# Four block sums of h moved from DVE to GpSimd, with a new order of all steps, in a two-layer graph attention kernel

## The chip, the core and the metric

The kernel runs on one core of a Trainium2 chip. The metric is the device time of one execution in microseconds (us); the kernel before took 2622.17 us, the median of 3 runs (2616.54 to 2627.53). The engines are TensorE (PE; its weight loads are shown as PEld), VectorE (DVE), ScalarE (ACT), GpSimd (POOL) and SyncE (SP), which issues most DMAs. Each engine runs its own queue in order and waits on semaphores for the others.

## The reference

x is 64 graphs of 256 nodes with 512 features, adj a 256 x 256 matrix of zeros and ones.

```python
h = maximum(layernorm(x), 0)
q, k, v = h @ Wq + bq, h @ Wk + bk, h @ Wv + bv          # 8 heads of 64
scores = einsum('bihd,bjhd->bhij', q, k) / 8 + where(adj == 0, -1e9, 0)
x = x + einsum('bhij,bjhd->bihd', softmax(scores), v)    # layer 0
h = maximum(layernorm(x), 0)
q, k, v = h @ Wq1.T, h @ Wk1.T, h @ Wv1.T
rel = adj.T * (q @ k.T)
x = x + (rel / norm(rel, axis=2)) @ v                    # layer 1
```

## The kernel before, in words

The 64 graphs are worked on as 32 pairs (512 rows, four tiles of 128 each). Every fp32 operand of a product is split in two fp16 halves, high and low, and a product is three matmuls (high·high, high·low, low·high) where one would do. ACT makes the high half, then another engine subtracts it from the fp32 value: for h, the probabilities and the projections that is POOL.

The three projections of layer 0 ("q", "k", "v") use a scheme with seven products of half-size blocks where plain tiling has eight. For it h, which lies in `x_in` as four quarters a11, a12, a21, a22, gives seven blocks: three are quarters, four are sums of quarters. `h_sum` makes those four in place, one after the other, as `ln0_sum` 0 to 3: a22 = a21 + a22, a21 = a11 - a21, a11 = a22 - a11, a12 = a12 - a11. Sum 0 may run when the low half of block 4 (the old a22) is made, sum 1 when all four tiles are normalised, sum 2 after the low half of block 0, sum 3 after that of block 1. Each quarter is 128 x 512 fp32 as one instruction. The seven splits (`ln0_split` 0 to 6, in the block order 4, 0, 1, 2, 3, 5, 6) take high halves on ACT (L578), low halves on POOL (L501) and a DMA transpose into `h0t` from SP (L411). There are three places for the halves (`HALVES`), so split n waits for the transpose of split n-3.

Layer 0's attention has 16 units a pair (head and graph): scores on PE (L991, four groups of four units), "mask" on DVE (L837), "exp" and the high half on ACT (L645, L653), the low half on POOL (L523), a transpose by SP (L454), and "pv" on PE. After every four units DVE divides ("norm", L851) and POOL adds the result to x ("residual", L539). `residual` 0 waits until DVE has added the bias to all four tiles ("biased", L893). Layer 1 has the products "rv", "rq" (four each, 12 matmuls of 512 columns), "rel" and "out"; ACT takes the high half of rv and rq (L661) and DVE the low one (L859). All products of a pair except scores and pv share three PSUM banks `B` in turn, so a product waits until the product three before it has left its bank; for rv and rq that is the DVE instruction L859.

What stands where is decided by tables of slots. A pair starts every 26 slots (`PERIOD`); the tables give each step of a pair its slot, negative ones for the steps that run ahead of the pair's own period and ones above 26 for those that run in the next. `timetable` picks the tables of a pair (the first two and the last three have some of their own), and `in_order` sorts all steps into `TENSOR_PLAN` (PE) and `PLAN`. DVE, ACT, POOL and SP each walk through the same `PLAN` and take the steps that are theirs:

```python
                elif kind == "ln0_sum" and p > 0:
                    h_sum(n, p)
```

So in any period PE works on the projections of pair p, the attention of p and p-1 and layer 1 of p-1 and p-2, while h of pair p+1 is being made.

Of the kernel before, what the change touches and what calls it, by code (L numbers as in the profile page):

```python
# [5 lines left out]
def adjacency_attention_two_layers(  # L6
# [74 lines left out]
    LAYER1 = {"ln1_stats": [38, 38.25, 38.5, 38.5], "ln1_power": [38.75], "ln1_scale": [39.5],
              "ln1_apply": [41, 41, 41.25, 41.5], "ln1_split": [41, 41.25, 41.5, 41.75], "squares": [55.75, 59.25],
              "rel_scale": [56, 60], "rel_split": [57, 60.75]}
# [3 lines left out]
    OPENING = {("rq", 0): 2, ("rq", 1): 3, ("rq", 2): 4, ("rq", 3): 5}  # L87

    TURNED_AT = {("rv", 0): 19, ("rv", 1): 20, ("rv", 2): 21, ("rv", 3): 22, ("rel", 0): 28}


    PRODUCT_0 = {("q", 0): 0, ("q", 1): 1.3, ("q", 2): 1.6, ("q", 3): 2.5, ("q", 4): 3.5, ("q", 5): 4.5, ("q", 6): 5,
                 ("k", 0): 5.5, ("k", 1): 5.55, ("k", 2): 5.85, ("k", 3): 6.75, ("k", 4): 7.25, ("k", 5): 8,
                 ("k", 6): 8.5, ("v", 0): 11.25, ("v", 1): 11.55, ("v", 2): 12.35, ("v", 3): 13.75, ("v", 4): 14.5,
                 ("v", 5): 15.75, ("v", 6): 16}
# [971 lines left out]
```

## Time and profile before

| | before |
|---|---|
| median of 3 runs | 2622.17 us (2616.54 to 2627.53) |
| the profiled execution's own time | 2622.53 us |
| its span in the profile | 2620.7 us |
| PE busy | 2353.5 us (90%) |
| DVE busy | 2077.3 us (79%) |
| ACT busy | 1754.4 us (67%) |
| POOL busy | 1763.9 us (67%) |
| mean granted TensorE clock | 0.974 |

The span runs from the first to the last instruction; 1.8 us of the execution lie outside it. PE is the busiest engine, but a share averages over stages: what ends a wait in one stage is seen in the timeline of that stage. One pair takes some 79 us and the 32 overlap, so that nearly all of the span is one pattern, repeated.

### The profile page before, as it was taken

What the parts mean: (1) busy time and instruction counts of PE and PEld (TensorE: products, weight loads), DVE (VectorE), ACT (ScalarE), POOL (GpSimd) and SP (SyncE); (2) the same over time, 40 slices, a digit from 0 to 9 for tenths busy, and PEclk for the clock granted to TensorE, in tenths of its full rate; (3) what the DMA queues carried; (4) which work ended last, traced back from release to release, by engine and by line L of the source; (5) the groups of instructions that cost most, each with busy time, mean ns of one, the idle gap of its engine ahead of it and who ended that gap; (6) DMA issues with size and microseconds to landing.
All of it is one profiled execution on the core that took longest, in us unless ns stands there. A gap on an engine that the chain in (4) does not pass through costs nothing.

```text
span 2620.7 us, 62396 instructions
## 1 busy us (share of the span) xinstructions
PE 2353.5 (90%) x22708; PEld 1644.8 (63%) x22708; DVE 2077.3 (79%) x5261; ACT 1754.4 (67%) x4318; POOL 1763.9 (67%) x1511
## 2 busy tenths in 40 slices
PE   5789999998999899999889999999999999999996
PEld 3656676666676665666656766666766656766663
DVE  6778877788888788877788887888787888787863
ACT  3676766776666676666666766666666766766762
POOL 2767776767676766766666766676676776666761
PEclk8899999999999999999999999999999999999998
DMA  5666766776777676666766766766666866766752
GB/s 165 126 129 130 143 139 131 138 150 130 139 148 126 137 151 129 138 137 123 149 133 136 147 126 130 153 132 139 146 128 132 156 132 138 146 128 131 142 120 66
DMA packets 1040353, 354.87 MB, mean 135 GB/s; under 512 B 987440, under 2 KB 987696, under 8 KB 1040048
## 3 DMA queue, kind: packets, MB, share of 16 engines
q1 hardware_dynamic: 1037264, 345.65, 65.6%
q10 hardware_dynamic: 2784, 5.24, 0.5%
q8 instruction: 180, 2.95, 0.5%
q14 instruction: 125, 1.02, 0.1%
HBM read 73.93 MB, written 33.55 MB: 41 GB/s over the span
## 4 chain that ended last, share of the span: by engine, by line
DVE 38%; PE 37%; issue 9%; POOL 6%; ACT 4%; DMA 2%; DVEq 0%; SPq 0%; ACTq 0%
PE B L908 33%; DVE whole L817 4%; DVE stats L707 4%; DVE rel_halves L871 3%; DVE probs L837 3%; DVE u L828 3%; DVE ln_work L695 2%; PE O L908 2%; DVE x_in L735 2%; PE S L991 2%; DVE x_in L739 2%; DVE x_in L743 2%; POOL x_res L539 2%; POOL halves L523 1%; DVE ln_work L699 1%
## 5 line engine op out<-in xcount | busy, mean ns | idle before, releaser
L523 POOL TENSOR_TENSOR halves<-probs,halves 128x512 f16<-128x512 f32 x512 | 618.7, 1211 | 325.5 <-ACT halves L653 322.5
L645 ACT ACTIVATE probs<-probs,neg_max 128x256 f32<-128x256 f32 x1024 | 506.8, 496 | 280.8 <-DVE neg_max L837 280.8
L908 PE MATMUL B<-h1t,wm 128*128 128x512 f16 x1488 | 371.0, 403 | 85.0 <-DVE rv L859 85.0
L501 POOL TENSOR_TENSOR h_halves<-x_in,h_halves 128x512 f16<-128x512 f32 x224 | 298.9, 1340 | 146.3 <-ACT h_halves L578 146.3
L908 PE MATMUL B<-wvt,h1t 128*128 128x512 f16 x1488 | 339.0, 380 | 51.7 <-DVE rv L859 34.6
L837 DVE CUSTOM_DVE_ANT_0 probs<-S,mask 128x256 f32<-128x256 f32 x1024 | 379.6, 416 | 5.5 <-PE S L991 2.6
L908 PE MATMUL B<-h0t,wq 128*128 128x256 f16 x2688 | 329.2, 275 | 24.5 <-ACT u L625 15.0
L653 ACT ACTIVATE halves<-probs 128x512 f16<-128x512 f32 x512 | 322.7, 630 | 16.2
L908 PE MATMUL B<-h0t,wk 128*128 128x256 f16 x2688 | 309.0, 273 | 11.5 <-DVE rel L865 11.5
L908 PE MATMUL B<-wv,h0t 128*128 128x256 f16 x2688 | 314.9, 273 | 1.3 <-DVE u L828 1.3
L908 PEld LDWEIGHTS B<-h1t,wm 128*128 128x128 f16 x1488 | 143.9, 103 | 267.4 <-DVE rv L859 99.8
L908 PEld LDWEIGHTS B<-h0t,wq 128*128 128x128 f16 x2688 | 256.1, 99 | 62.1 <-ACT u L625 15.3
L908 PEld LDWEIGHTS B<-wv,h0t 128*128 128x128 f16 x2688 | 257.7, 98 | 50.3 <-issue 7.0
L908 PEld LDWEIGHTS O<-v,probs_t 128*128 128x128 f16 x6144 | 237.2, 99 | 82.0 <-POOL v L520 17.4
L908 PEld LDWEIGHTS B<-h0t,wk 128*128 128x128 f16 x2688 | 256.3, 98 | 48.2 <-DVE rel L865 19.8
L908 PEld LDWEIGHTS B<-wvt,h1t 128*128 128x128 f16 x1488 | 138.4, 98 | 226.2 <-DVE rv L859 49.4
L908 PE MATMUL O<-v,probs_t 128*128 128x64 f16 x6144 | 255.5, 194 | 16.0 <-POOL v L520 6.3
L828 DVE TENSOR_TENSOR u<-B,u 128x512 f32<-128x512 f32 x288 | 196.6, 683 | 62.9 <-PE B L908 62.8
L539 POOL TENSOR_TENSOR x_res<-x_res,attn 128x512 f32<-128x512 f32 x124 | 157.7, 1272 | 98.7 <-DVE x_res L893 55.4
L908 PE MATMUL B<-rv,rel_t 128*128 128x512 f16 x768 | 190.8, 386 | 30.8 <-DVE u L828 21.9
L508 POOL TENSOR_TENSOR h_halves<-h,h_halves 128x512 f16<-128x512 f32 x128 | 148.5, 1160 | 101.1 <-ACT h_halves L592 101.0
L991 PE MATMUL S<-k_st,q_st 64*128 64x256 f16 x3072 | 191.7, 271 | 25.9 <-DVE neg_max L837 25.6
(114 smaller groups left out, 4090.2 us busy)
## 6 DMA issues: line engine op xcount, KB each, us to landing
x_in<-in_x_dram SPq DMA_DIRECT2D x132, 256.0 KB, 3.9
out_dram<-result SPq DMA_DIRECT2D x128, 256.0 KB, 3.4
x_res<-in_x_dram SPq DMA_DIRECT2D x124, 256.0 KB, 3.2
probs_t<-halves SPq DMA_TRANSPOSE x512, 2.9
h0t<-h_halves SPq DMA_TRANSPOSE x228, 3.2
h1t<-h_halves SPq DMA_TRANSPOSE x124, 3.7
rq<-in_L_gnn_Wq_dram ACTq DMA_DIRECT2D x4, 256.0 KB, 5.1
x_res<-in_L_gnn_Wk_dram ACTq DMA_DIRECT2D x4, 256.0 KB, 5.8
```

The costliest lines, as they stand in the source:

```text
L501: nc.gpsimd.tensor_tensor(halves_by_column(step, 1), by_column(h_block(SPLIT_ORDER[n])), halves_by_column(step, 0), ALU.subtract).then_inc ...
L508: nc.gpsimd.tensor_tensor(h_halves[:, place, 1, :], h[:, n % 2, :], h_halves[:, place, 0, :], ALU.subtract).then_inc(h_low[1], 1)
L523: nc.gpsimd.tensor_tensor(halves[:, n % RING, 1, :], probs[:, (UNITS * p + n) % SOFT, :, :].rearrange("p t n -> p (t n)"), halves[:, n % R ...
L539: nc.gpsimd.tensor_tensor(cols, cols, attn[:, :, :].rearrange("p (t e) d -> p t (e d)", e=2), ALU.add).then_inc(residual, 1)
L645: ins = nc.scalar.activation(probs[:, soft, i, :], probs[:, soft, i, :], ACT.Exp, bias=neg_max[:, soft, i:i + 1], scale=-1.0, accum_out=ro ...
L653: nc.scalar.activation(halves[:, n % RING, 0, :], probs[:, (UNITS * p + n) % SOFT, :, :].rearrange("p t n -> p (t n)"), ACT.Copy).then_inc ...
L707: ins = nc.vector.bn_stats(stats[:, layer, t, :], src[:, t, :])
L817: ins = nc.vector.scalar_tensor_tensor(whole[:, c % 2, t, :], now[:, t, :], b[:, f + t:f + t + 1], before[:, t, :], ALU.add, ALU.add)
L828: nc.vector.tensor_tensor(u[:, 1 if n == 3 else 0, :, :].rearrange("p t n -> p (t n)"), product[:, :], before, ALU.add).then_inc(u_done, 1)
L837: ins = nc.vector.tensor_tensor_reduce(out=probs[:, soft, i, :], in0=S[n % 4][:, i, :], in1=mask[:, i, :], scale=SCORE, scalar=BIG, op0=AL ...
L908: ins = nc.tensor.matmul(dst, left(i), right(j), start=(n == 0), stop=(n == len(pairs) - 1))
L991: ins = nc.tensor.matmul(S[2 * g + e][:, i, :], q_st[own, n, hq, col(g * NT + i)], k_st[own, n, hk, col(g, N)], start=(t == 0), stop=(t == ...
```

## The change

`h_sum` is taken out of DVE's part and made a helper that takes the engine. The four sums of the first pair, in the setup, are still called on DVE; those of all other pairs are issued by POOL, at their place in `PLAN`. The waits of each sum are the same as before. The slots of nearly every step change in the tables for all pairs, for the first two and for the last three. The tables `OUT_29`, `PRODUCT_30` and so on of the last three pairs keep the old numbers or get new ones, where before they repeated those of all pairs.

```diff
-    SCORED = [8.75, 12.75, 20.0, 26.5]
-    MASKED = [9, 12, 16.25, 19, 23.0, 25.5, 29, 31]
+    SCORED = [8.25, 13.75, 22.0, 28.0]
+    MASKED = [9, 12, 16.0, 19.75, 23.75, 26.0, 27.5, 30]
...
-              "ln0_apply": [-8.5, -8.25, -7.5, -7.25], "ln0_sum": [-7, -7, -6.5, -5.25],
+              "ln0_scale": [-9], "ln0_apply": [-8.5, -8, -7.5, -7.25], "ln0_sum": [-7, -7, -6.5, -4.25],
...
+        def h_sum(eng, engine, n, pair):
+
+            a11, a12, a21, a22 = [quarter(x_in, i, j) for i in range(2) for j in range(2)]
+            low = BLOCKS * pair + 1
+            if n == 0:
+                eng.wait_ge(h_low[0], low + SPLIT_ORDER.index(4))
+                ins = engine.tensor_tensor(a22, a21, a22, ALU.add)
...
+            ins.then_inc(summed_blocks, 1)
+
         @block.sync
...
                     ln_power(1, p + 1)
+                elif kind == "ln0_sum" and p > 0:
+                    h_sum(pool, nc.gpsimd, n, p)
                 elif kind == "ln0_split" and p > 0:
                     h0_low_half(n, p)
...
             for n in range(4):
-                h_sum(n, 0)
+                h_sum(dve, nc.vector, n, 0)
...
-                elif kind == "ln0_sum" and p > 0:
-                    h_sum(n, p)
```

Below, rows of the two programs' order of instructions, in the middle of the run. The line numbers of the changed kernel differ: L862 is the old L859, L894 the old L893, L847 the old L844, L523 the old L501, L545 the old L523, L563 the old L539, L909 the old L908, L992 the old L991; L413, L417, L421 and L425 are the four sums. DVE, where rv2, rv3 and rq0 leave their banks, before:

```order
L893 TENSOR_TENSOR x_res<-x_res,bv 128x512
L735 TENSOR_TENSOR x_in<-x_in 128x2x256
L739 TENSOR_TENSOR x_in<-x_in 128x2x256
L743 TENSOR_TENSOR x_in<-x_in 128x2x256
L893 TENSOR_TENSOR x_res<-x_res,bv 128x512
L859 TENSOR_TENSOR rv<-B,rv 128x512
L893 TENSOR_TENSOR x_res<-x_res,bv 128x512
L859 TENSOR_TENSOR rv<-B,rv 128x512
L747 TENSOR_TENSOR x_in<-x_in 128x2x256
L844 RECIPROCAL row_inv<-row_sum 128x8
L859 TENSOR_TENSOR rq<-B,rq 128x512
```

DVE at the same place, changed:

```order
L894 TENSOR_TENSOR x_res<-x_res,bv 128x512
L862 TENSOR_TENSOR rv<-B,rv 128x512
L894 TENSOR_TENSOR x_res<-x_res,bv 128x512
L862 TENSOR_TENSOR rv<-B,rv 128x512
L847 RECIPROCAL row_inv<-row_sum 128x8
L894 TENSOR_TENSOR x_res<-x_res,bv 128x512
L862 TENSOR_TENSOR rq<-B,rq 128x512 x2
```

The four sums are gone, one biased tile (x_res<-x_res,bv) stands ahead of each of rv2 and rv3 and one behind, and rq1's low half now stands ahead of the four masks that follow.

POOL from the first split of h to the residual, before (h_halves are low halves of h, halves those of the probabilities of units 6 and 7, the row with attn is residual 0):

```order
L501 TENSOR_TENSOR h_halves<-x_in,h_halves 128x512 x2
L523 TENSOR_TENSOR halves<-probs,halves 128x512
L501 TENSOR_TENSOR h_halves<-x_in,h_halves 128x512
L523 TENSOR_TENSOR halves<-probs,halves 128x512
L539 TENSOR_TENSOR x_res<-x_res,attn 128x4x128
L523 TENSOR_TENSOR halves<-probs,halves 128x512
L501 TENSOR_TENSOR h_halves<-x_in,h_halves 128x512
L523 TENSOR_TENSOR halves<-probs,halves 128x512
```

POOL at the same place, changed:

```order
L523 TENSOR_TENSOR h_halves<-x_in,h_halves 128x512
L413 TENSOR_TENSOR x_in<-x_in 128x2x256
L417 TENSOR_TENSOR x_in<-x_in 128x2x256
L523 TENSOR_TENSOR h_halves<-x_in,h_halves 128x512
L421 TENSOR_TENSOR x_in<-x_in 128x2x256
L523 TENSOR_TENSOR h_halves<-x_in,h_halves 128x512
L545 TENSOR_TENSOR halves<-probs,halves 128x512
L563 TENSOR_TENSOR x_res<-x_res,attn 128x4x128
L545 TENSOR_TENSOR halves<-probs,halves 128x512
L425 TENSOR_TENSOR x_in<-x_in 128x2x256
```

Three sums now stand ahead of unit 6 and the fourth behind unit 7, and the residual has moved up between the two units.

PE from rv0 to the unit behind rq3, before (wvt is a product rv, wm one of rq, O a unit of pv, S the scores):

```order
L908 MATMUL B<-wvt,h1t 128x512 x12
L908 MATMUL O<-v,probs_t 128x64 x12
L908 MATMUL B<-wvt,h1t 128x512 x36
L991 MATMUL S<-k_st,q_st 128x256 x24
L908 MATMUL O<-v,probs_t 128x64 x12
L908 MATMUL B<-h1t,wm 128x512 x24
L908 MATMUL O<-v,probs_t 128x64 x12
L908 MATMUL B<-h1t,wm 128x512 x12
L908 MATMUL O<-v,probs_t 128x64 x12
L908 MATMUL B<-h1t,wm 128x512 x12
L908 MATMUL O<-v,probs_t 128x64 x12
```

PE at the same place, changed:

```order
L909 MATMUL B<-wvt,h1t 128x512 x24
L909 MATMUL O<-v,probs_t 128x64 x12
L909 MATMUL B<-wvt,h1t 128x512 x24
L909 MATMUL B<-h1t,wm 128x512 x12
L909 MATMUL O<-v,probs_t 128x64 x12
L992 MATMUL S<-k_st,q_st 128x256 x24
L909 MATMUL B<-h1t,wm 128x512 x24
L909 MATMUL O<-v,probs_t 128x64 x24
L909 MATMUL B<-h1t,wm 128x512 x12
L909 MATMUL O<-v,probs_t 128x64 x12
```

The scores and one pv, which stood ahead of rq0, stand behind it now, and a pv has moved from between rq1 and rq2 to behind rq2.

PE at the very end of the program, before: the last pair's rv (wvt), rq (wm), rel and out.

```order
L908 MATMUL B<-wvt,h0t 128x512 x48
L908 MATMUL B<-h0t,wm 128x512 x48
L908 MATMUL B<-h0t,rq 128x256 x48
L908 MATMUL B<-rv,rel_t 128x512 x24
```

PE at the same place, changed:

```order
L909 MATMUL B<-h0t,wm 128x512 x48
L909 MATMUL B<-h0t,rq 128x256 x24
L909 MATMUL B<-wvt,h0t 128x512 x24
L909 MATMUL B<-h0t,rq 128x256 x24
L909 MATMUL B<-wvt,h0t 128x512 x24
L909 MATMUL B<-rv,rel_t 128x512 x24
```

The last pair takes rq first, and its rv in two parts behind each rel.

## Rows read from the trace of the kernel before

**Rows 1.** The page, parts 1 and 4: busy time; chain that ended last.

```profile
PE 2353.5 (90%) x22708; PEld 1644.8 (63%) x22708; DVE 2077.3 (79%) x5261; ACT 1754.4 (67%) x4318; POOL 1763.9 (67%) x1511
...
DVE 38%; PE 37%; issue 9%; POOL 6%; ACT 4%; DMA 2%; DVEq 0%; SPq 0%; ACTq 0%
```

**Rows 2.** Waits, 400 to 2400 us: waiting line <- releaser: us, times, longest.

```profile
PE B L908 <- DVE rv L859: 103.7, 50, 2.8
...
PE B L908 <- DMA h1t<-h_halves: 14.7, 28, 1.7
```

**Rows 3.** Timeline, PE, one pair: start us, us, line, tiles, [idle before].

```profile
1337.46 2.75 PE L908 MATMUL B<-wvt,h1t 128*128 128x512 f16 x12 [1.72 <-DMA h1t<-h_halves]
...
1347.04 2.76 PE L908 MATMUL B<-wvt,h1t 128*128 128x512 f16 x12 [1.29 <-DVE rv L859]
1350.35 1.49 PE L991 MATMUL S<-k_st,q_st 64*128 64x256 f16 x24 [0.55 <-DVE neg_max L837]
...
1357.72 2.76 PE L908 MATMUL B<-h1t,wm 128*128 128x512 f16 x12 [2.84 <-DVE rv L859]
...
1363.26 0.51 PE L908 MATMUL O<-v,probs_t 128*128 128x64 f16 x12
...
1372.00 0.51 PE L908 MATMUL O<-v,probs_t 128*128 128x64 f16 x12
```

**Rows 4.** Timeline, DVE, the same stretch.

```profile
1350.72 1.65 DVE L735 TENSOR_TENSOR x_in<-x_in 128x512 f32<-128x512 f32 x1
...
1355.42 1.64 DVE L893 TENSOR_TENSOR x_res<-x_res,bv 128x512 f32<-128x512 f32 x1
1356.98 0.68 DVE L859 TENSOR_TENSOR rv<-B,rv 128x512 f16<-128x512 f32 x1
```

**Rows 5.** The first sum by line: ns min/median/max, first and last start.

```profile
L735 DVE TENSOR_TENSOR x_in<-x_in x32: 679/1648/1651, 18.3 to 2452.4; 128x512 f32<-128x512 f32 x32
```

**Rows 6.** Groups by line: count | busy us, mean ns | idle before.

```profile
L539 POOL TENSOR_TENSOR x_res<-x_res,attn 128x512 f32<-128x512 f32 x124 | 157.7, 1272 | 98.7 <-DVE x_res L893 55.4 <-DVE attn L851 43.3
...
L893 DVE TENSOR_TENSOR x_res<-x_res,bv 128x512 f32<-128x512 f32 x124 | 115.3, 930 | 0.0
...
L735 DVE TENSOR_TENSOR x_in<-x_in 128x512 f32<-128x512 f32 x32 | 51.8, 1617 | 7.5 <-POOL h_halves L501 7.5
```

**Rows 7.** Timeline, POOL, the same stretch.

```profile
1347.70 1.16 POOL L501 TENSOR_TENSOR h_halves<-x_in,h_halves 128x512 f16<-128x512 f32 x1 [2.99 <-ACT h_halves L578]
...
1351.90 1.49 POOL L523 TENSOR_TENSOR halves<-probs,halves 128x512 f16<-128x512 f32 x1
...
1354.91 1.60 POOL L523 TENSOR_TENSOR halves<-probs,halves 128x512 f16<-128x512 f32 x1
1358.34 1.26 POOL L539 TENSOR_TENSOR x_res<-x_res,attn 128x512 f32<-128x512 f32 x1 [1.83 <-DVE x_res L893]
```

**Rows 8.** Timeline, DVE, a sum of the first pairs.

```profile
95.20 0.68 DVE L735 TENSOR_TENSOR x_in<-x_in 128x512 f32<-128x512 f32 x1
```

**Rows 9.** Transposes of the probabilities: ns in the SP queue; us to landing.

```profile
L454 SPq DMA_TRANSPOSE probs_t<-halves x512: 1231/1237/2549, 73.2 to 2554.9; - x171
...
DMA to landing us min/median/max: 2.7/2.9/6.8
```

**Rows 10.** Timeline, PE, the wait at rq1 in the first pair.

```profile
171.77 4.19 PE L908 MATMUL B<-h1t,wm 128*128 128x512 f16 x12 [2.84 <-DVE rv L859]
```

**Rows 11.** Two windows: busy us (x) by engine, PEclk, DMA share, GB/s.

```profile
171.00:176.00 5.00, 4.23 (x20) 1.74 (x21) 5.00 (x14) 0.63 (x2) 3.61 (x3) 0.66 0.37 76
1357.00:1362.00 5.00, 4.28 (x31) 2.17 (x32) 5.00 (x14) 0.63 (x3) 3.66 (x3) 1.00 0.45 92
```

**Rows 12.** Timeline, PE, the last pair's products.

```profile
2574.01 12.31 PE L908 MATMUL B<-wvt,h0t 128*128 128x512 f16 x48 [9.54 <-DMA h0t<-h_halves]
...
2598.19 5.40 PE L908 MATMUL B<-h0t,rq 128*128 128x256 f16 x48 [1.51 <-DVE rq L859]
2609.27 8.27 PE L908 MATMUL B<-rv,rel_t 128*128 128x512 f16 x24 [5.68 <-issue]
```

More of the change, by code:

```diff
@@ L81, in adjacency_attention_two_layers @@
[L81 to L95, printed above, removed]
@@ new lines, in adjacency_attention_two_layers @@
+    LAYER0 = {"x_in": [-25, -24.25, -24.25, -19.25], "ln0_stats": [-14.25, -12, -11.75, -9.5], "ln0_power": [-10],
+              "ln0_scale": [-9], "ln0_apply": [-8.5, -8, -7.5, -7.25], "ln0_sum": [-7, -7, -6.5, -4.25],
+              "ln0_split": [-7.5, -6.5, -6.5, -4, -3.25, 0.25, 0.75], "x_res": [7.5, 12.25, 15.25, 15.25],
+              "biased": [18, 20.5, 21, 22], "residual": [20, 24.75, 31.5, 35.5]}
+    LAYER1 = {"ln1_stats": [38, 38.25, 38.25, 38.25], "ln1_power": [38.5], "ln1_scale": [39.25],
+              "ln1_apply": [41, 41, 41.5, 41.75], "ln1_split": [41, 41.25, 41.5, 41.75], "squares": [54.75, 59.5],
+              "rel_scale": [56, 60], "rel_split": [57, 60.5]}
@@ new lines, in adjacency_attention_two_layers @@
+    OPENING = {('rq', 0): 2, ('rq', 1): 3, ('rq', 2): 4, ('rq', 3): 5}
+    TURNED_AT = {('rv', 0): 19.0, ('rv', 1): 19.25, ('rv', 2): 20.25, ('rv', 3): 24.5, ('rel', 0): 25.75}
+    PRODUCT_0 = {("q", 0): 0, ("q", 1): 1.05, ("q", 2): 1.35, ("q", 3): 2.25, ("q", 4): 3.25, ("q", 5): 3.5,
[3 rows of a table added]
+    SCORED_0 = [8.5, 13.0, 21.25, 27.0]
+    MASKED_0 = [9.25, 12, 15.5, 20.0, 23.25, 25.75, 27.5, 30.25]
+    MULTIPLIED_0 = [14.5, 15, 16.25, 16.25, 22, 22.25, 23.75, 25.25, 28.75, 29, 30, 31, 34, 34.25, 35.5, 35.5]
@@ new lines, in adjacency_attention_two_layers @@
+    LAYER0_0 = {"x_res": [10.75, 11.5, 12.5, 13.25], "biased": [16.75, 19.25, 20.75, 22.75],
+                "residual": [22.75, 25.5, 32, 35.5]}
+    PRODUCT_1 = {("q", 0): -2, ("q", 1): -0.2, ("q", 2): 0.35, ("q", 3): 2.25, ("q", 4): 2.25, ("q", 5): 4.5,
[3 rows of a table added]
+    LAYER0_1 = {"x_in": [-24, -23.75, -22.75, -22.25], "ln0_stats": [-16.75, -12.75, -12.75, -10], "ln0_power": [-10],
+                "ln0_scale": [-9.5], "ln0_apply": [-9, -8.75, -8, -7.5], "ln0_sum": [-7.5, -6.75, -6, -4.75],
+                "ln0_split": [-8, -7, -6.25, -3.75, -3, -2, 0.25]}
@@ L117, in adjacency_attention_two_layers @@
                   ("k", 6): 8.5, ("v", 0): 11.25, ("v", 1): 11.55, ("v", 2): 12.35, ("v", 3): 13.75, ("v", 4): 14.5,
[2 rows of a table removed]
-                  ("rel", 1): 56.75, ("out", 0): 61, ("out", 1): 62.5, ("out", 2): 66.75, ("out", 3): 67.25}
[2 rows of a table added]
+                  ("out", 0): 53, ("out", 1): 54, ("out", 2): 55, ("out", 3): 56}
     SCORED_31 = [8.75, 12.75, 20.0, 26.5]
@@ L404, in need @@
                 eng.wait_ge(semaphore, value)
+        def h_sum(eng, engine, n, pair):
[4 more added lines that the diff above has]
+                ins = engine.tensor_tensor(a22, a21, a22, ALU.add)
+            elif n == 1:
+                eng.wait_ge(ln_done[0], TILES * (pair + 1))
+                eng.wait_ge(summed_blocks, 4 * pair + 1)
+                ins = engine.tensor_tensor(a21, a11, a21, ALU.subtract)
+            elif n == 2:
+                eng.wait_ge(h_low[0], low + SPLIT_ORDER.index(0))
+                eng.wait_ge(summed_blocks, 4 * pair + 2)
+                ins = engine.tensor_tensor(a11, a22, a11, ALU.subtract)
+            else:
+                eng.wait_ge(h_low[0], low + SPLIT_ORDER.index(1))
+                eng.wait_ge(summed_blocks, 4 * pair + 3)
+                ins = engine.tensor_tensor(a12, a12, a11, ALU.subtract)
+            ins.then_inc(summed_blocks, 1)
         @block.sync
```

54 lines of the change are left out of this document (10 added, 44 removed), and 18 rows, old and new, of tables (PRODUCT_0, PRODUCT_1, PRODUCT_31, PRODUCT_AT).

## The prediction

> **What bounds the kernel now.** I read the page first. PE is busy 90% of the span, DVE 79%, and the chain that ended last lies on these two in equal parts, 38% on DVE and 37% on PE [rows 1]. So PE's work sets most of the time and DVE the rest; the question is where PE waits. The list of waits answers it: from 400 to 2400 us PE waited 103.7 us, in 50 waits, for the DVE instruction that takes rv's low half out of its bank, and 14.7 us for the transposes of layer 1's h; nothing else comes near [rows 2].
>
> The timeline of one pair shows where that is. PE waits 1.72 us ahead of rv0, 1.29 ahead of rv3, 0.55 ahead of the third group of scores and 2.84 at 1357.72 ahead of rq1 [rows 3]. That last one needs the bank of rv2. DVE starts rv2's low half only at 1356.98, and ahead of it stand three of the four block sums, from 1350.72 to 1355.42, and one biased tile of 1.64 [rows 4]. So the sums stand in the one stretch in which PE waits for DVE. The length of a pair comes from the same wait, which is at 171.77 in the first pair [rows 10] and at 1357.72 fifteen pairs later: 1185.95 / 15 = 79.06 us. It occurs 30 times: the first sum is there 32 times [rows 5], of which one is in the setup and one, the second pair's, has no layer 1 beside it.
>
> **What the change removes.** On DVE a sum takes 1.62 us in the mean [rows 6] and 1.65 beside a busy POOL, against 0.68 where nothing is in its way [rows 4, 8]. Gone are at most 4 x 1.65 = 6.6 us a pair of DVE, and 4.7 of it ahead of rv2. DVE would come to rv2 after one biased tile, at 1350.7 + 1.64 = 1352.4, and the bank would be free at 1353.1. PE, without the waits of 0.55 and 2.84, comes to rq1 at 1357.72 - 3.39 = 1354.33. The wait of 2.84 goes, with 1.2 us to spare. The 0.55 goes as well, since these scores now stand behind rq0 and one pv, 3 us later, and the masks that they wait for don't. **Term 1: -3.39 us a pair**, between -3.39 and -1.7 (if ACT, whose high half of rv2 comes first, delays it by half).
>
> **What it adds.** POOL has no row for such a sum. The nearest is residual, same shape, fp32 out: 1.27 us in the mean [rows 6]; a low half takes 1.16 alone and 1.49 to 1.60 beside DVE's sums [rows 7]. I take 1.27; the ends are 1.16 and 1.65. POOL is not idle enough for it to be free everywhere. What stands behind the sums on POOL are the low halves of the probabilities, then SP's transposes, then pv on PE.
>
> - Unit 6. Before, its low half ends at 1351.90 + 1.49 = 1353.39, and PE wants it at 1363.26 [rows 3, 7]: plenty. Changed, POOL has four low halves and three sums to make from 1347.70 on, and the first split stands behind rv1's high half on ACT, some 0.55 later. 1347.70 + 0.55 + 4 x 1.16 + 3 x 1.27 = 1356.70, and 0.44 more for each of two biased tiles that come between (1.60 against 1.16): 1357.6. The transpose lands 2.9 us after its issue [rows 9], at 1360.5. PE now comes there at 1363.26 - 3.39 = 1359.87. A new wait of 0.6.
> - Unit 8. Behind unit 6 POOL has the residual, unit 7, the fourth sum, two splits and unit 8: 2 x 1.27 + 4 x 1.16 = 7.18, with one more tile of DVE between 7.62. That is 1365.2, landing at 1368.1, or 1369.4 if SP is still issuing the one ahead, 1.24 each [rows 9]. PE came there at 1372.00 [rows 3]; it now comes 3.39 earlier, without the last scores (1.42 from the row of 1.49) ahead of it, and 0.6 later again: 1367.8. A new wait of 0.3 to 1.6; I take 0.8.
>
> **Term 2: +1.4 us a pair.** The lower end: nothing contends, unit 6 lands at 1356.70 + 2.9 = 1359.6 and unit 8 at 1366.8, both ahead of PE: 0. The upper end: every POOL instruction takes 1.60. Unit 6 ends at 1347.70 + 0.55 + 7 x 1.60 = 1359.45 and lands at 1362.35 (wait 2.5), unit 8 six instructions later at 1369.05, landing at 1371.95 against 1369.7 (2.3): +4.8.
>
> DVE also pays: its biased tiles take 0.93 in the mean and 1.64 beside POOL [rows 4, 6]. If all four meet the busier POOL that is 4 x 0.71 = 2.8 us a pair, less than half of what it was relieved of, and the tile ahead of rv2 is in the sum above.
>
> What speaks against the move is a rule of the Trainium skill (GPSIMD Engine Reference, Engine selection): elementwise work on two inputs belongs on VectorE, as GpSimd is about twice as slow. In this trace 1.27 stands against 0.68, the ratio the page gives, but in the place where the sums stand DVE takes 1.65. By the page a sum would be 2 x 0.68 = 1.36, which makes term 2 larger by under 0.4. The 1.65 agrees with the SBUF page (Who interferes with whom): a DVE instruction with two SBUF inputs and a GpSimd one that reads SBUF exclude each other, and the later fully waits.
>
> **Term 3, the clock.** In the first pair the 12 matmuls behind the wait of 2.84 took 4.19 us, with a granted clock of 0.66 in that window; fifteen pairs later, behind the same wait, 2.76 at 1.00 [rows 3, 10, 11]. So such a wait can cost up to 1.43 us more, in some pairs and not in others. With no wait of that length left, part of it comes back: between 0 and -1.43; **I take -0.6 us a pair**.
>
> **The rest of the order.** From rq1 to rv0 PE has no wait of over a microsecond, and the new slots there trade places of products and pv; I see nothing that removes the waits of 1.72 ahead of rv0 and 1.29 ahead of rv3, which hang on the layer-norm chain. I take 0, with ends of -1 and +1 a pair. The first two pairs: 0, with 4 us to both sides.
>
> **The last pair.** Before, rv starts at 2574.01, as soon as the first of four tiles is transposed; rel waits 1.51 and out 5.68, and the 24 matmuls of out take 8.27 [rows 12], against 5.2 at the rate of the steady pairs (12 matmuls of the same width take 2.6 of the 2.75 that the row of rq shows, 0.216 each) [rows 3]. Changed, rq goes first and needs all four tiles: three more transposes of 1.24 and some waiting for the three places, 3.7 to 5 us later, say 4.3. In exchange rv fills the wait for rel's halves: 5.68 less 1 that I leave, and out at the full rate, 3.1. Together 4.3 - 4.7 - 3.1 = -3.5, between -8 and +4.
>
> **The sum.** -3.39 + 1.4 - 0.6 = -2.59 a pair, x 30 = -77.7, and -3.5 at the end: -81.2. The profiled execution took 2622.53 us (its span is 2620.7, the rest lies outside it), 0.4 from the median of 2622.17. 2622.5 - 81.2 = 2541.3. **I predict 2541 us**, about 3% faster.
>
> **Rivals.**
>
> *POOL hides the sums.* Term 2 is 0 and the clock gives back all: -3.39 - 1.43 = -4.82 a pair, 2622.5 - 144.6 - 3.5 = 2474; with half of the clock's part, 2496. For it: POOL is 67% busy and waited 1.83 us ahead of the residual alone [rows 1, 7]. Against it: the sums stand in its densest stretch. Between 2474 and 2510.
>
> *The wait only moves.* rq1 no longer waits, but another chain that runs once round a pair sets its length: residual 3, layer 1's stats, its transposes (the 1.72 ahead of rv0) or the scale chain behind rv3's 1.29, both of which pass through DVE instructions that a busier POOL lengthens. If 0.5 us of 3.39 is left: 2622.5 - 15 - 3.5 = 2604; if nothing, 2619. For it: DVE and PE share the chain evenly [rows 1]. Against it: both of these waits begin far behind rq1, and 14.7 us in 25 pairs is the smaller part [rows 2].
>
> *POOL becomes the bound: slower.* Three sums and the residual stand ahead of unit 7, and the residual waits on POOL until the fourth biased tile, which now stands behind rv3's low half on DVE. If POOL's instructions are all of 1.60, term 2 is +4.8: -3.39 + 4.8 = +1.4 a pair, x 30 = +42, and 2622.5 + 42 - 3.5 = 2661. It decides from the point where units 6 and 8 together cost PE more than 3.4 us, that is where POOL is 2.9 us later than I have it. For it: 1.60 was measured beside DVE's sums. Against it: just those are gone.
>
> That the order does not change is excluded by the rows of both programs.
>
> **How the numbers follow.** My forecast's case has 62%, with a range of its own of 2515 to 2570 (1 us a pair to either side). POOL hides the sums: 13%. The wait moves: 15%, half of it above 2604. POOL bounds: 10%. The range for 8 in 10 goes from 2488 to 2604: it leaves out the slower rival, half of the moved wait and the lowest part of the first rival, 19% together. Half a per cent, 13 us, is about what a measurement here can tell. Faster by more: 62 + 13 + 8 = 83%. Within it: 7 of the moved wait and 1 of the last, 8%. Slower: 9%.
>
> **What would show it.** Right: the wait for rv's bank ahead of rq1 is gone, while those ahead of rv0 and rv3 stay; four sums a pair on POOL of about 1.27 us; new waits of under a microsecond of pv for the transposes of the probabilities; a pair of 76.5 us; fewer stretches of lower granted clock; a last out without the wait of 5.68. Wrong: pv waits of 2 us and more (term 2), sums on POOL of 1.6 and more, a pair still of 78 to 79 us with longer waits ahead of rv0 or rv3, or new waits of the projections for a bank, since I took 0 for all the other moves.

## The result

The changed kernel took **2539.66 us**, the median of 4 runs (2537.17 to 2541.73). The kernel before took 2620.98 in the same comparison (4 runs, 2616.54 to 2627.53). The ratio is 0.9687, with a 95% interval of 0.9665 to 0.971: about 3% faster. The prediction was 2541, with a range of 2488 to 2604.

The profiled execution took 2541.73 us, with a span of 2539.9. The page, parts 1 and 4, to be laid beside [rows 1]:

```profile
PE 2327.8 (92%) x22708; PEld 1645.1 (65%) x22708; DVE 1899.1 (75%) x5137; ACT 1755.9 (69%) x4318; POOL 1877.2 (74%) x1635
...
PE 34%; DVE 25%; POOL 18%; issue 9%; DMA 7%; ACT 5%; SPq 2%; ACTq 0%; DVEq 0%; POOLq 0%
```

POOL has the 124 instructions that DVE lost, and 113 us more to do; DVE has 178 less. Of the chain that ended last 18% now lie on POOL, where it was 6%. PE is busy 26 us less with the same 22708 matmuls, as the mean granted clock rose from 0.974 to 0.985.

PE's waits from 400 to 2300 us, a stretch of 24.9 pairs (waiting line <- releaser: us, times, longest):

```profile
PE O L909 <- DMA probs_t<-halves: 42.7, 40, 2.8
PE B L909 <- DVE rv L862: 30.0, 25, 1.4
...
PE B L909 <- DMA h1t<-h_halves: 18.1, 33, 2.1
```

Before, the first of these was not there and the second stood at 103.7 us, in 50 waits over 2000 us [rows 2]. One pair on PE (start us, us, tiles, [idle before]), against [rows 3]:

```profile
1298.25 5.34 PE L909 MATMUL B<-wvt,h1t 128*128 128x512 f16 x24 [1.58 <-DMA h1t<-h_halves]
...
1307.83 2.76 PE L909 MATMUL B<-wvt,h1t 128*128 128x512 f16 x12 [1.30 <-DVE rv L862]
1310.43 2.75 PE L909 MATMUL B<-h1t,wm 128*128 128x512 f16 x12
1313.02 0.51 PE L909 MATMUL O<-v,probs_t 128*128 128x64 f16 x12
1313.47 1.48 PE L992 MATMUL S<-k_st,q_st 64*128 64x256 f16 x24
1314.88 5.35 PE L909 MATMUL B<-h1t,wm 128*128 128x512 f16 x24
...
1321.49 0.52 PE L909 MATMUL O<-v,probs_t 128*128 128x64 f16 x12 [0.91 <-DMA probs_t<-halves]
```

The waits ahead of rv0 (1.58, was 1.72) and rv3 (1.30, was 1.29) stay. Those ahead of the third scores and of rq1 are gone: rq0, pv, the scores and then rq1 and rq2 run without a gap. The new one is ahead of pv of unit 6. POOL in the same stretch, against [rows 7]:

```profile
1308.83 1.16 POOL L523 TENSOR_TENSOR h_halves<-x_in,h_halves 128x512 f16<-128x512 f32 x1 [3.33 <-ACT h_halves L602]
1310.07 1.27 POOL L413 TENSOR_TENSOR x_in<-x_in 128x512 f32<-128x512 f32 x1
1311.49 1.54 POOL L417 TENSOR_TENSOR x_in<-x_in 128x512 f32<-128x512 f32 x1
...
1314.22 1.70 POOL L421 TENSOR_TENSOR x_in<-x_in 128x512 f32<-128x512 f32 x1
...
1317.00 1.61 POOL L545 TENSOR_TENSOR halves<-probs,halves 128x512 f16<-128x512 f32 x1
1318.56 1.26 POOL L563 TENSOR_TENSOR x_res<-x_res,attn 128x512 f32<-128x512 f32 x1
```

From split 0 (1308.83) to the end of unit 6's low half (1318.61) POOL does seven instructions with hardly a gap. The residual behind them no longer waits for the biased tiles, as it did for 1.83. Three sums and DVE's biased tile in the groups by line, against [rows 6] (count | busy us, mean ns | idle before):

```profile
L894 DVE TENSOR_TENSOR x_res<-x_res,bv 128x512 f32<-128x512 f32 x124 | 112.3, 905 | 0.0
...
L421 POOL TENSOR_TENSOR x_in<-x_in 128x512 f32<-128x512 f32 x31 | 52.9, 1705 | 2.4
L417 POOL TENSOR_TENSOR x_in<-x_in 128x512 f32<-128x512 f32 x31 | 47.4, 1530 | 4.3
L413 POOL TENSOR_TENSOR x_in<-x_in 128x512 f32<-128x512 f32 x31 | 39.5, 1274 | 2.4
```

On DVE, before, these four sums took 51.8, 46.2, 45.7 and 42.4 us in 32 instructions each, 1.45 us in the mean. On POOL the four groups together (the last one 39.2 us) have a mean of 1.44: in their own places the sums are as long on one engine as on the other.

**Where the 80.8 us of span went.** The first sum of the third pair starts at 164.77 before and at 163.14 after, that of the last one at 2452.36 and at 2372.4: 78.88 and 76.18 us a pair, 2.70 less, 78.3 over 29 pairs. The head gives 1.6, and what follows the last sum 0.8 (168.3 and 167.5). So nearly all of it is in the pairs.

### The profile page after: what moved, and what is told of

It is laid out like the page before. It is cut to its first block, busy times and chain, and to the rows that moved or that the text cites. A ratio compares the mean times of both kernels' runs of the same rounds, so it can differ in the third digit from the quotient of the medians.

```text
span 2539.9 us, 62396 instructions
## 1 busy us (share of the span) xinstructions
PE 2327.8 (92%) x22708; PEld 1645.1 (65%) x22708; DVE 1899.1 (75%) x5137; ACT 1755.9 (69%) x4318; POOL 1877.2 (74%) x1635
## 3 DMA queue, kind: packets, MB, share of 16 engines
q14 instruction: 126, 1.03, 0.2%
## 4 chain that ended last, share of the span: by engine, by line
PE 34%; DVE 25%; POOL 18%; issue 9%; DMA 7%; ACT 5%; SPq 2%; ACTq 0%; DVEq 0%; POOLq 0%
PE B L909 29%; DMA probs_t<-halves 5%; DVE stats L731 4%; POOL h_halves L523 4%; POOL halves L545 3%; PE O L909 3%; DVE ln_work L721 3%; DVE ln_work L719 3%; POOL x_res L563 3%; DVE probs L840 2%; DVE u L831 2%; POOL x_in L421 2%; PE S L992 2%; POOL x_in L417 2%; SPq L434 2%
## 5 line engine op out<-in xcount | busy, mean ns | idle before, releaser
L545 POOL TENSOR_TENSOR halves<-probs,halves 128x512 f16<-128x512 f32 x512 | 607.4, 1187 | 185.4 <-ACT halves L677 183.0
L909 PE MATMUL B<-wvt,h1t 128*128 128x512 f16 x1488 | 337.7, 380 | 55.4 <-DVE rv L862 34.7
L909 PE MATMUL B<-h0t,wq 128*128 128x256 f16 x2688 | 325.3, 276 | 26.1 <-ACT u L649 15.4
L523 POOL TENSOR_TENSOR h_halves<-x_in,h_halves 128x512 f16<-128x512 f32 x224 | 258.1, 1164 | 114.1 <-ACT h_halves L602 114.1
L909 PE MATMUL B<-h1t,wm 128*128 128x512 f16 x1488 | 339.7, 382 | 0.0
L909 PEld LDWEIGHTS O<-v,probs_t 128*128 128x128 f16 x6144 | 233.5, 98 | 148.4 <-DMA probs_t<-halves 58.8
L909 PE MATMUL O<-v,probs_t 128*128 128x64 f16 x6144 | 259.8, 194 | 69.5 <-DMA probs_t<-halves 63.6
L909 PE MATMUL B<-wv,h0t 128*128 128x256 f16 x2688 | 310.2, 273 | 0.1
L909 PE MATMUL B<-h0t,wk 128*128 128x256 f16 x2688 | 304.1, 273 | 0.3 <-DVE whole L820 0.3
L909 PEld LDWEIGHTS B<-h0t,wq 128*128 128x128 f16 x2688 | 256.9, 99 | 58.7 <-ACT u L649 15.7
L909 PEld LDWEIGHTS B<-wvt,h1t 128*128 128x128 f16 x1488 | 139.0, 98 | 229.0 <-DVE rv L862 49.5
L909 PEld LDWEIGHTS B<-wv,h0t 128*128 128x128 f16 x2688 | 257.5, 98 | 43.6 <-issue 7.0
L909 PEld LDWEIGHTS B<-h0t,wk 128*128 128x128 f16 x2688 | 260.5, 98 | 30.6 <-DVE whole L820 0.6
L909 PEld LDWEIGHTS B<-h1t,wm 128*128 128x128 f16 x1488 | 141.6, 98 | 169.3 <-issue 9.9
L831 DVE TENSOR_TENSOR u<-B,u 128x512 f32<-128x512 f32 x288 | 197.1, 684 | 51.8 <-PE B L909 50.8
L542 POOL TENSOR_TENSOR k_st<-whole,k_st 128x512 f16<-128x512 f32 x128 | 151.1, 1180 | 89.7 <-ACT k_st L660 89.7
L909 PE MATMUL B<-rv,rel_t 128*128 128x512 f16 x768 | 188.1, 382 | 25.2 <-DVE u L831 24.1
L992 PE MATMUL S<-k_st,q_st 64*128 64x256 f16 x3072 | 192.2, 272 | 9.8 <-DVE neg_max L840 8.2
```

Source lines behind the costliest of these rows:

```text
L523: nc.gpsimd.tensor_tensor(halves_by_column(step, 1), by_column(h_block(SPLIT_ORDER[n])), halves_by_column(step, 0), ALU.subtract).then_inc ...
L542: nc.gpsimd.tensor_tensor(dst(1), whole[:, c % 2, :, :], dst(0), ALU.subtract).then_inc(whole_low, 1)
L545: nc.gpsimd.tensor_tensor(halves[:, n % RING, 1, :], probs[:, (UNITS * p + n) % SOFT, :, :].rearrange("p t n -> p (t n)"), halves[:, n % R ...
L831: nc.vector.tensor_tensor(u[:, 1 if n == 3 else 0, :, :].rearrange("p t n -> p (t n)"), product[:, :], before, ALU.add).then_inc(u_done, 1)
L909: ins = nc.tensor.matmul(dst, left(i), right(j), start=(n == 0), stop=(n == len(pairs) - 1))
L992: ins = nc.tensor.matmul(S[2 * g + e][:, i, :], q_st[own, n, hq, col(g * NT + i)], k_st[own, n, hk, col(g, N)], start=(t == 0), stop=(t == ...
```

## The experiments

All were run in three rounds beside the kernel before, which took 2618.93, 2619.17 and 2627.47 us in its three comparisons. So a difference of a few us between two versions of different rounds says little by itself. The waits quoted are all of PE, from 400 to 2300 us. The diffs are cut to the lines that matter; `...` marks what is left out.

### The two parts of the change apart

**New slots, sums on DVE.** The changed kernel with the sums back on their old engine:

```diff
-                elif kind == "ln0_sum" and p > 0:        # in POOL's walk through PLAN
-                    h_sum(pool, nc.gpsimd, n, p)
+                elif kind == "ln0_sum" and p > 0:        # in DVE's
+                    h_sum(dve, nc.vector, n, p)
```

> The changed kernel with all its new slots, but the four sums back on DVE. My theory (the sums belong off DVE, the slots only make room): on DVE sums 0 to 2 now stand ahead of the masks of units 6 and 7 and of rv2's low half, 4.7 us of them, so PE waits 2 to 4 us a pair at the third scores or at rq1, and the time is 2590 to 2660 us. Rival (the new slots carry the gain, the engine is nothing): 2540 us, within 10.

Measured: 2605.07 us (2599.15 to 2606.37), ratio 0.994 (0.9919 to 0.9961). The new slots alone bring 14 of the 80 us.

```profile
PE S L992 <- DVE neg_max L838: 54.1, 25, 2.2
```

The long wait is still there, once a pair, and has moved: it is ahead of the third scores (2.17 us at 1344.85), which wait for masks. On DVE these stand behind sum 2, and sum 2 behind POOL:

```profile
1341.70 1.63 DVE L421 TENSOR_TENSOR x_in<-x_in 128x512 f32<-128x512 f32 x1 [1.05 <-POOL h_halves L523]
1343.25 0.41 DVE L838 CUSTOM_DVE_ANT_0 probs<-S,mask 128x256 f32<-128x256 f32 x1
```

The rival, that the new order makes the gain by itself, falls. It is less the length of the sums that holds DVE up here: the four take 117.7 us in this trace, 0.92 each, against 186.1 before. DVE also stands idle 31.4 us for POOL ahead of sum 2, with the masks behind it.

**Old slots, sums on POOL.** The reverse: the tables of the kernel before with the sums in POOL's walk.

```diff
-    LAYER0 = {... "ln0_sum": [-7, -7, -6.5, -4.25],
-              "ln0_split": [-7.5, -6.5, -6.5, -4, -3.25, 0.25, 0.75], ...
+    LAYER0 = {... "ln0_sum": [-7, -7, -6.5, -5.25],
+              "ln0_split": [-8, -7, -6.5, -4, -3.25, -2.25, 0], ...      # and all other tables of before
```

> The kernel before with all its old slots, the four sums on POOL. My theory: PE's wait of 2.84 us ahead of rq1 is gone, the 0.55 ahead of the third scores stays, and POOL takes back under 1 us a pair as two of the sums stand ahead of unit 6 and three ahead of unit 7: 2550 to 2575 us. Rival (the new slots carry the gain): 2610 to 2622 us, with another wait in the place of the one removed.

Measured: **2522.01 us** (2519.52 to 2522.65), ratio 0.9625 (0.9593 to 0.9657). That is below the expected range, and 17.7 faster than the changed kernel. The engine move alone brings 97 us; the new slots, worth 14 with the sums on DVE, cost 17.7 once they are on POOL. Its waits:

```profile
PE B L908 <- DVE rv L861: 41.5, 50, 1.4
...
PE S L991 <- DVE neg_max L839: 14.7, 27, 0.6
...
PE O L908 <- DMA probs_t<-halves: 0.4, 2, 0.3
```

Pv waits 0.4 us in all. The reason stands on POOL:

```profile
1300.17 1.58 POOL L416 TENSOR_TENSOR x_in<-x_in 128x512 f32<-128x512 f32 x1
1301.72 1.60 POOL L522 TENSOR_TENSOR h_halves<-x_in,h_halves 128x512 f16<-128x512 f32 x1
1303.28 1.15 POOL L544 TENSOR_TENSOR halves<-probs,halves 128x512 f16<-128x512 f32 x1
1304.40 1.26 POOL L420 TENSOR_TENSOR x_in<-x_in 128x512 f32<-128x512 f32 x1
```

Unit 6's low half (L544) comes ahead of the third sum and its split; in the changed kernel it comes behind both. It ends 17.1 us after the start of rv0 here and 20.4 there, while PE comes to unit 6 some 22 to 23 us after it in both. The price is a wait of 0.37 us ahead of rq1 and the old 0.55 ahead of the third scores. Together its waits are 94.7 us against 113.1, and a pair is (2352.6 - 96.0) / 30 = 75.22 us long, against (2372.4 - 93.0) / 30 = 75.98 with the same count in the changed kernel.

**Sums later on DVE.** The kernel before, in which the sums stay on DVE but stand behind rv3's low half:

```diff
-"ln0_sum": [-7, -7, -6.5, -5.25]
+"ln0_sum": [-5.2, -5.15, -5.1, -5.05]
```

> The kernel before, sums on DVE, with their slots alone moved behind rv3's low half. My theory, that rq1 waits only because the sums stand ahead of rv2: the 2.84 us are gone, but the sums now stand ahead of the masks of units 8 and 9 and hold up ACT's splits 3 to 6, which takes back 1 to 2 us a pair: 2565 to 2605 us. Rival (DVE simply has too much work, so that it must go to another engine): 2615 us or more.

Measured: 2588.39 us (2587.61 to 2588.75), ratio 0.988 (0.9848 to 0.9912).

```profile
PE S L991 <- DVE neg_max L837: 37.9, 50, 1.0
PE B L908 <- DVE rv L859: 35.2, 46, 1.4
```

The wait for rv, 96.6 us in this stretch of the kernel before, is down to 35.2 without POOL's help: it was the sums' place ahead of rv2. But DVE is as full as before and hands the time to the scores, in pieces of a microsecond or less. The place alone is worth 31 us; the other 66 of the 97 take the other engine. Of the 31 much is clock, not waiting: the group of rq matmuls went from 371.0 to 341.9 us, while all waits together went only from 152.4 to 135.9.

### POOL's order and load

**Unit 6 first.** If pv's wait is the order on POOL, unit 6's low half ahead of split 1, sum 2 and split 2 should end it:

```diff
-    MASKED = [9, 12, 16.0, 19.75, 23.75, 26.0, 27.5, 30]
+    MASKED = [9, 12, 16.0, 19.25, 23.75, 26.0, 27.5, 30]
```

> The changed kernel with the slot of the masks of units 6 and 7 at 19.25 where it had 19.75, so that on POOL unit 6's low half stands ahead of one split, the third sum and another split, and unit 7's behind the residual as before. My theory, that PE's new waits of 0.9 us and more ahead of pv of unit 6 come from what stands ahead of it on POOL: they go, and the time falls by 1 to 1.5 us a pair to 2495 to 2515 us. Rival (the waits are transposes that queue on SP or collide, whatever POOL's order): 2535 to 2545 us, the waits where they were.

Measured: 2546.43 us (2540.73 to 2548.19), ratio 0.9713 (0.9692 to 0.9734). A miss by 31, near the rival's time, but not for its reason.

```profile
PE B L909 <- DVE rv L862: 52.6, 47, 1.4
...
PE O L909 <- DMA probs_t<-halves: 19.5, 25, 2.2
```

pv's wait halves (42.7 to 19.5), and rv's grows by the same (30.0 to 52.6): a new one of 0.82 us stands ahead of rq1. The order on POOL was indeed the cause at unit 6. In the changed kernel some 31 of the 42.7 us are ahead of unit 6; here none of the 19.5 is: 14.8 are ahead of unit 8 and the rest ahead of unit 7. The sum of all waits is 114.1 against 113.1. On DVE, rv2's low half now waits 3.35 us for ACT's high half:

```profile
1316.86 0.69 DVE L862 TENSOR_TENSOR rv<-B,rv 128x512 f16<-128x512 f32 x1 [3.35 <-ACT rv L685]
```

In the changed kernel ACT makes it at 1312.90, between the exponentials of units 6 and 7, and DVE waits 1.62; here it comes behind both, at 1316.25. One slot put right does not take the wait out: the slot moves the unit on every engine, and the wait changes places.

**Spare work on POOL, new slots.** Three additions of 128 x 128 a pair ahead of split 1's low half, into a tile that nobody reads:

```diff
+                    if n == 1:
+                        for part in range(3):
+                            need(pool, spare_done, 3 * (p - 1) + part)
+                            nc.gpsimd.tensor_tensor(spare[:, :], ident[:, :], ident[:, :],
+                                                    ALU.add).then_inc(spare_done, 1)
                     h0_low_half(n, p)
```

> The changed kernel with three spare additions of 128x128 on POOL for each pair, ahead of the second split of h, which compute nothing that is used (about 1.3 us of POOL a pair, taken from the 0.29 us of the 128x128 select in the setup and the semaphore between them). My theory (POOL is what PE waits for in this stretch): the 1.3 us come out nearly whole in the waits of pv, +30 to +42 us: 2570 to 2582 us. Rival (POOL has room left): 2540 to 2550 us.

Measured: 2607.76 us (2604.62 to 2612.47), ratio 0.9953 (0.9936 to 0.997), 68 above the changed kernel. The 93 additions took 37.1 us (399 ns each).

```profile
PE O L916 <- DMA probs_t<-halves: 68.9, 26, 3.8
```
```profile
1510.07 0.82 PE L916 MATMUL O<-v,probs_t 128*128 128x64 f16 x12 [2.58 <-DMA probs_t<-halves]
1510.70 4.11 PE L916 MATMUL B<-h1t,wm 128*128 128x512 f16 x12
```
```profile
1510.00:1515.00 5.00, 4.93 (x37) 2.49 (x38) 0.69 (x1) 2.60 (x8) 3.72 (x4) 0.66 0.71 142
```

pv waits 68.9 us in 24.3 pairs, against 42.7 in 24.9: 1.12 more a pair, 34 over thirty. The other half is the clock: behind the wait the 12 matmuls take 4.11 us, with a granted clock of 0.66 in those 5 us (the third value from the end; part at 1.2 GHz, which is 0.5, and part at 2.4), where they take 2.75 at 1.00. The group of all rq matmuls went from 339.7 to 373.5 us, +33.8. The mechanism was as expected, its size was not (26 us above the range): the clock had been left out. Behind unit 6's wait the 12 matmuls of rq3 were slow, 3.94 us or more instead of 2.75, in 21 of 25 pairs here; in the changed kernel in 2 of 25.

**The same, twice instead of three times.**

```diff
-                        for part in range(3):
+                        for part in range(2):
```

> The changed kernel with two spare additions a pair in place of three (0.8 us of POOL a pair by the 399 ns that one took). Three cost 68 us, 2.3 a pair, for 1.2 us of work; rq's matmuls took 34 us longer in all with it, 409 ns in place of 382. My theory (the rest is the clock, which falls behind a wait of PE of over 2 us): 0.8 x 30 = 24 us of waits and a smaller share of slow stretches, 2565 to 2590 us, with rq's matmuls between 382 and 409. Rival (the cost is in proportion, each addition 23 us): 2585 us, with rq's matmuls at 400.

Measured: 2576.34 us (2572.88 to 2578.83), ratio 0.9813 (0.9775 to 0.9851), +36.7. pv waits 57.1 us, the rq group takes 367.1 us (404 ns a matmul). The 12 matmuls of rq3 were slow in 16 of 25 pairs. The first two additions cost 18.3 us each and the third, 12.4 us of POOL, another 31.4: the time is in the theory's range, and the rival's even 23 each does not hold. The theory's words on waits of over 2 us go further than the traces: in the changed kernel the wait of 2.38 at 555.75 was followed by slow matmuls and that of 2.20 at 633.54 was not.

**Spare work on POOL, old slots.** The same three additions in the kernel with the old slots and POOL's sums.

> The same spare additions in the kernel with the old slots and the sums on POOL (2522 us). There PE waited 0.4 us in 25 pairs for the probabilities. My theory (under the old slots unit 6 stands further up on POOL and PE comes to it behind one product fewer, so there is room): under +10 us, 2522 to 2532 us. Rival (POOL is as tight there): +30 us, 2550 us or more.

Measured: 2562.2 us (2561.93 to 2562.27), ratio 0.9777 (0.9756 to 0.9797), 40 above its own base.

```profile
L559 POOL TENSOR_TENSOR spare<-ident 128x128 f32<-128x128 f32 x93 | 50.4, 542 | 4.9
...
L915 PE MATMUL B<-h1t,wm 128*128 128x512 f16 x1488 | 341.6, 379 | 11.1 <-DVE rv L868 11.1
```
```profile
PE S L998 <- DVE neg_max L846: 39.7, 49, 1.2
```

50.4 us of POOL's work, 40 of the span: POOL has no room under the old slots either, and that theory falls. It reaches PE by way of the scores (14.7 to 39.7 us, none over 1.2), and the rq matmuls stay at 379 ns. So the same load costs 28 us less here. The clock's part of the other, some 34 us, is near that.

### Giving one sum back to DVE

If POOL sets the pace, one sum less should bring something.

```diff
-                elif kind == "ln0_sum" and p > 0:
+                elif kind == "ln0_sum" and p > 0 and n not in (3,):      # POOL
+                elif kind == "ln0_sum" and p > 0 and n in (3,):          # DVE
+                    h_sum(dve, nc.vector, n, p)
```

**Sum 3, old slots with the new end:**

> The best so far (old slots, sums on POOL, new slots for the last two pairs, 2518.7 us) with the fourth sum back on DVE, where it stands behind rv3's low half and no longer ahead of anything that PE waits for at rq1. My theory, after the spare load showed POOL to set the pace in this stretch under either slots: 1.27 us a pair come off POOL and most of it off the time, 2485 to 2500 us. Rival (the load acted through its place ahead of unit 6 alone, and the fourth sum stands behind unit 7): 2515 to 2522 us. A second rival (DVE takes it back, since the sum takes 1.4 us there beside POOL): 2525 us or more.

Measured: 2531.33 us (2530.65 to 2533.73), ratio 0.9648 (0.9616 to 0.9679), 13 slower than with it on POOL (2518.66, the version with the new end, below). The theory missed by 31; the second rival had it.

```profile
L424 DVE TENSOR_TENSOR x_in<-x_in 128x512 f32<-128x512 f32 x32 | 51.2, 1600 | 15.8 <-POOL h_halves L522 15.7
```

On DVE the sum takes 1600 ns, more than the 1270 on POOL, and DVE idles 15.7 us ahead of it. PE's waits for the masks went from 14.6 to 23.2 us.

**Sum 3, new slots:**

> The changed kernel (2539.7 us) with the fourth sum back on DVE. The waits of pv come at unit 6, ahead of the fourth sum on POOL, and at unit 8 and 9, behind it. If POOL's whole chain sets the pace: 2505 to 2520 us. If only what stands ahead of unit 6 does: the small waits at unit 8 go, 2532 to 2540 us.

Measured: 2534.7 us (2532.71 to 2538.02), ratio 0.966 (0.9628 to 0.9692), 5 below the changed kernel with ranges that touch: not clear. It stood behind unit 6 on POOL, and pv waits 39.6 instead of 42.7. POOL's whole chain does not set the pace. The time fits the second expectation, but its reason does not: the waits at unit 8 stay, up to 1.62 us.

**Sum 1, old slots with the new end** (`n in (1,)`):

> As the first of these, but with the second sum on DVE instead of the fourth, which puts 1.65 us of DVE back ahead of rv2's low half and takes 1.5 off POOL ahead of unit 6. If POOL paces: 2490 to 2505 us. If rv2's place on DVE is what counts: the wait ahead of rq1 grows by about a microsecond, 2530 to 2550 us.

Measured: 2516.92 us (2516.15 to 2520.25), ratio 0.9594 (0.9562 to 0.9625), the same as with it on POOL (2518.66).

```profile
L895 DVE TENSOR_TENSOR x_res<-x_res,bv 128x512 f32<-128x512 f32 x124 | 143.3, 1156 | 0.0
...
L416 DVE TENSOR_TENSOR x_in<-x_in 128x512 f32<-128x512 f32 x32 | 52.4, 1638 | 1.3 <-POOL x_in L412 1.2
```

Neither the gain nor the loss that was expected: POOL is spared 1570 ns a pair, and DVE has 1638 more to do. Biased tiles take 1156 ns here and 1103 with all four sums on POOL.

### The end

**The new end undone:** the changed kernel with the old tables for its last two pairs (`PRODUCT_30`, `PRODUCT_31` and their `LAYER1` tables back to the values for all pairs).

```diff
-... ("rv", 0): 48, ("rv", 1): 49, ("rv", 2): 51, ("rv", 3): 52, ("rq", 0): 43, ...
+... ("rv", 0): 42.75, ("rv", 1): 43.5, ("rv", 2): 45.25, ("rv", 3): 45.75, ("rq", 0): 47.75, ...
```

> The changed kernel with the slots of the last two pairs as in the kernel before (rv first, rel in its old place). The prediction gave the new end -3.5 us, so this should take 3.5 us more, 2543 us. Rival, from the two traces (from the last pair's last scores to the end 80.1 us before and 80.3 changed): the new end brings nothing, 2540 us, within 1 us.

Measured: 2542.34 us (2537.57 to 2545.44), against 2539.66 (2537.17 to 2541.73): the ranges overlap, so the times alone decide nothing.

**The new end on the old slots:**

> The kernel with the old slots and the sums on POOL, but the slots of the last two pairs as in the changed kernel. The undoing of the new end in the changed kernel gave 2542.3 against 2539.7, which the intervals hardly tell from nothing. If the new end brings what I predicted: 2518 us. If nothing: 2522 us.

Measured: **2518.66 us** (2518.13 to 2521.18), ratio 0.9613 (0.9595 to 0.963), against 2522.01 (2519.52 to 2522.65): 3.3 below, with ranges that overlap. From the last scores to the end of the span it is 77.95 us, against 79.99 with the old end.

That difference does not hold across the traces. This last stretch took 79.1 to 80.1 us in the five traces with the old end, and 77.7 to 81.2 in the nine with the new one; the version with sum 1 on DVE has the same end as this one and 80.07. The means are 79.7 and 79.1. In these means the new end is worth 0.6 us, less than its own scatter.

This kernel and the version with sum 1 on DVE are the fastest of all, 21 and 23 us below the changed kernel.

## Why the prediction was right

**The bound and the place.** Right. The sums ahead of rv2 on DVE made the wait at rq1: moving them behind rv3 on the same engine takes all waits for rv from 96.6 to 35.2 (400 to 2300 us). One reading was off: 1.62 us is the mean of the first sum alone. The four have 1.45, so 5.8 us a pair went from DVE, not up to 6.6. The sum of the terms does not use it. The wait went with 0.7 us to spare, not 1.2: rv2's low half ends at 1314.20 and rq1 starts at 1314.88, as DVE waits 1.62 for ACT's high half.

**Term 1, -3.39 a pair.** Right in sum. In the list of waits, rv went from 96.6 us in 24.1 pairs (400 to 2300, before) to 30.0 in 24.9, 4.01 to 1.20 a pair, and the scores from 13.7 to nothing, 0.57 a pair: -3.38.

**Term 2, +1.4.** pv's new waits are 42.7 / 24.9 = 1.71 a pair; right in kind, 0.3 small. POOL's row from the start of split 0 to the end of unit 6 was 9.3 us in the prediction and 9.8 measured: not two meetings with DVE, 0.88 together, but three, at sums 1 and 2 and at unit 6 (0.27 + 0.43 + 0.45 = 1.15), and 0.18 of gaps. Split 0 started 0.34 later behind rv0 than before, where 0.55 was taken, which gives a part of it back. In this pair unit 6 waits 0.91 where 0.6 was worked out, but single pairs are much worse, with 2.81 us at 1167.81, and unit 8 waits 0.15 here and up to 2.11 elsewhere, where 0.8 was taken. Over the stretch some 31 of the 42.7 us are unit 6's, 1.25 a pair, and 0.46 the others'. The rule of the Trainium skill (GPSIMD Engine Reference, Engine selection) is that GpSimd is about twice as slow as VectorE on two inputs. The trace agrees for undisturbed tiles, 1.27 us for the last sum against 0.68, and 2 x 0.68 would give 1.36. Yet beside a busy POOL DVE's mean was 1.45 against POOL's 1.44, and moving only the engine is worth 97 us.

**DVE's biased tiles** did not get longer: 905 ns against 930 [rows 6]. Costing them at nothing was right for the new slots; under the old ones they take 1103.

**Term 3, the clock, -0.6.** Right in kind, too small: with term 2 this is the part that was mis-sized. The group of rq matmuls that stands behind the wait:

```profile
L909 PE MATMUL B<-h1t,wm 128*128 128x512 f16 x1488 | 339.7, 382 | 0.0
```

Before, it took 371.0 us (403 ns each): -31.3, or -1.04 a pair. The trace of before already held this number. The prediction compared two pairs; over all 30 the wait ahead of rq1 is 2.83 or 2.84 us, and the 12 matmuls behind it take 2.76 in 12 pairs and 4.05 to 5.30 in 18, 29.2 us more in all, 0.97 a pair. So "up to 1.43 us" was too low for a single pair as well:

```profile
1035.65 5.30 PE L908 MATMUL B<-h1t,wm 128*128 128x512 f16 x12 [2.84 <-DVE rv L859]
```

In those 6 us the granted clock was 0.50, 1.2 GHz throughout. Why equal waits are followed by either clock stays open. A little is not given back after the change, as the longest of pv's waits have the same effect, in 2 of 25 pairs:

```profile
555.75 0.52 PE L909 MATMUL O<-v,probs_t 128*128 128x64 f16 x12 [2.38 <-DMA probs_t<-halves]
556.12 4.44 PE L909 MATMUL B<-h1t,wm 128*128 128x512 f16 x12
```

**The rest of the order, 0.** The waits for u, h1t and h0t moved by +0.07, +0.12 and +0.07 a pair, and that of rel, 0.39 a pair before, went away. In the list that is inside the 1 us to both sides. But the order as a whole is not worth 0, which only the experiments show: it gives 14 us with the sums on DVE and costs 17.7 with them on POOL. The prediction gave the move and the slots one answer. Its term 2, 1.71 a pair as measured, is the price of the order: unit 6 stands behind three splits and three sums on POOL, and under the old slots pv's waits are 0.02 a pair. It did not ask what the old slots would have made of it.

**The parts together.** -3.38 + 1.71 - 1.04 + 0.07 + 0.12 + 0.07 - 0.39 = -2.84, against -2.70 measured; predicted -2.59. Term 2 was short by 0.3 and term 3 by 0.4, on opposite sides. That the total comes within 1.3 us of the forecast, with the last pair off by 3.7 as well, is luck in part.

**The last pair, -3.5.** The step that failed. The out wait of 5.68 [rows 12] went, as was said:

```profile
2500.55 13.07 PE L909 MATMUL B<-h0t,wm 128*128 128x512 f16 x48 [14.92 <-DMA h0t<-h_halves]
...
2533.99 2.75 PE L909 MATMUL B<-rv,rel_t 128*128 128x512 f16 x12 [0.51 <-issue]
```

From the first product to the end it is 39.35 us, against 46.7 before. But that product starts 40.9 us after the last scores, against 33.4, so 7.5 later, not the 4.3 taken for it. Together 80.26 against 80.06: nothing gained in the trace. In the other traces with the new end the first product comes 39.1 to 42.1 us after the last scores, with the old end 32.9 to 33.7: 5.5 us later at least. The term to blame is this 4.3, the wait for four tiles in place of one.

**The rivals.** "POOL hides the sums" is out: pv waits 1.71 us a pair, and spare work on POOL shows in the time, 68 and 40 us. "The wait only moves" was wrong for this change and right for the next step: it is what happened when unit 6 was put first. "POOL becomes the bound" came true in its place, behind split 0, with half of the 3.4 us that would have decided. Its "2.9 us later" does not follow from the prediction's own terms: 0.6 + 0.8 reach 3.4 when POOL is 2.0 later.

**Left open.** Why sum 1 costs the same on either engine; why the order that ends unit 6's waits gives all of it back at rq1, unit 7 and unit 8; and, of the 28 us between the spare work under the two orders, how much is the clock beside the waits, since with two additions the waits and the rq group together (18 + 27) say some 8 us more than was measured.

## What to carry to other kernels

Where an engine is the one waited for in one stretch of a loop, moving work off it there pays even to a slower engine; work out what is queued behind it on the new engine, and time the move and the new order apart, for here the move alone was worth more than both. Here, when an engine had no room, a better place for one step only handed its wait on. Idle time of PE in many short waits was cheaper here than in one piece, which cost clock as well. What a wait costs in clock is read from every pair of the trace, not from one or two.
